# Order of the first steps in a fused attention, router and expert kernel

## What is computed

```python
n  = layernorm(x)                                   # used as a factor on the scores
qp = ctx @ Wq.T + bq;  kp = ctx @ Wk.T + bk         # (4, 512, 128)
s  = (qp @ kp.T) * H ** -0.5 * n                    # (4, 512, 512)
s  = where(mask | key_padding_mask, -inf, s)
x  = x + softmax(s)
t  = layernorm(x).reshape(2048, 512)
shared = silu(t @ sg) * (t @ su) @ sd               # inner width 256
top_val, top_idx = top_k(t @ router_w, 2)
p  = sigmoid(top_val) at top_idx, else 0
out = sum over experts e of (silu(p_e*t @ gate_e) * (p_e*t @ up_e)) @ down_e
x  = x + shared + out
```

## Time and profile before

| what | us |
|---|---|
| median of 3 runs | 363.01 |
| lowest and highest | 361.55, 363.92 |
| the profiled execution | 363.71 |
| its span, first to last instruction | 362.0 |

### The profile page before, as it was taken

How to read it: one execution, slowest core, us unless ns; L and a number is a source line. 1 busy time by engine, 2 the same in 40 slices (tenths; PEclk the granted TensorE clock), 3 DMA queues, 4 the chain that set the end, 5 groups by cost and what they waited for, 6 DMA issues and landing times.

```text
span 362.0 us, 6464 instructions
## 1 busy us (share of the span) xinstructions
PE 318.5 (88%) x1601; PEld 218.8 (60%) x1627; DVE 210.0 (58%) x461; ACT 177.9 (49%) x400; POOL 230.9 (64%) x199
## 2 busy tenths in 40 slices
PE   2866999999999983628999989999999999999991
PEld 1333666676767762315776757777777777777760
DVE  0766789999998789612444334444444444444441
ACT  2477767757767736102644434444444444444440
POOL 0688999986774749958385554756555465555433
PEclk9989899999999998587999999999999999999997
DMA  7956777857556320075346465867666566675736
GB/s 178 308 197 211 206 228 254 247 194 230 205 162 210 124 89 0 0 199 164 68 82 111 72 116 111 131 113 130 108 116 115 115 120 117 91 133 88 132 36 83
DMA packets 29764, 50.61 MB, mean 140 GB/s; under 512 B 5473, under 2 KB 9313, under 8 KB 29729
## 3 DMA queue, kind: packets, MB, share of 16 engines
q0 software_dynamic: 9008, 21.66, 33.5%
q1 hardware_dynamic: 19232, 27.99, 24.6%
q10 hardware_dynamic: 1488, 0.54, 0.8%
HBM read 30.45 MB, written 19.73 MB: 139 GB/s over the span
## 4 chain that ended last, share of the span: by engine, by line
PE 56%; DMA 11%; issue 11%; POOL 9%; DVE 7%; ACT 4%; POOLq 1%; ACTq 0%; DVEq 0%
PE bank L949 10%; PE bank L959 9%; PE bank L954 9%; DMA out_rows<-y,jscatter 9%; PE bank L982 5%; PE bank L988 5%; PE bank L985 5%; PE bank L1073 4%; PE bank L968 3%; POOL gu_lo L356 2%; PE bank L912 2%; POOL pen L351 2%; DMA kpad_in<-in_mask_BxS_bf 2%; PE bank L921 1%; POOL rstd L332 1%
## 5 line engine op out<-in xcount | busy, mean ns | idle before, releaser
L439 POOL DMA_INDIRECT out_rows<-y,jscatter x39 | 61.9, 1588 | 73.3 <-DMA out_rows<-y,jscatter 47.1
L959 PE MATMUL bank<-gu_hi,x_lo 128*128 (+1 forms) x220 | 70.3, 441 | 0.0
L949 PE MATMUL bank<-gu_hi,x_hi 128*128 (+1 forms) x220 | 63.0, 409 | 3.4 <-POOL dn_lo L356 1.4
L671 DVE TENSOR_TENSOR x_lo<-bank,x_hi 128x512 fp32r<-128x512 f32 x55 | 37.9, 690 | 33.1 <-ACT x_bf L507 33.0
L954 PE MATMUL bank<-gu_lo,x_bf 128*128 (+1 forms) x201 | 54.8, 387 | 1.3 <-issue 0.2
L864 DVE SCALAR_TENSOR_TENSOR h<-bank,xg,h 128x256 f32<-128x256 f32 x39 | 18.9, 484 | 57.8 <-ACT h L595 57.8
L420 POOL DMA_INDIRECT xg<-xn_rows,jgather x39 | 41.7, 1069 | 15.5 <-issue 15.5
L514 ACT CAST h_hi<-bank 128x256 fp32r<-128x256 f32 x55 | 20.6, 375 | 59.6 <-PE bank L968 59.4
L959 PEld LDWEIGHTS bank<-gu_hi,x_lo 128*128 128x128 f32 x220 | 41.7, 190 | 12.8 <-issue 0.6
L356 POOL TENSOR_TENSOR gu_lo<-stage,gu_hi 128x1024 bf16<-128x1024 f32 x18 | 43.3, 2405 | 9.6 <-ACT gu_hi L493 9.6
L949 PEld LDWEIGHTS bank<-gu_hi,x_hi 128*128 128x128 f32 x220 | 41.0, 193 | 13.6 <-issue 3.0
(11 more groups left out here) (128 smaller groups left out, 497.5 us busy)
## 6 DMA issues: line engine op xcount, KB each, us to landing
stage<-in_L_ffn_gate_up_w SPq DMA_DIRECT2D x16, 512.0 KB, 3.8
xin<-in_x SPq DMA_DIRECT2D x16, 256.0 KB, 4.3
xn_rows<-xn SPq DMA_DIRECT2D x16, 256.0 KB, 4.0
stage<-in_L_ffn_down_w SPq DMA_DIRECT2D x8, 512.0 KB, 3.8
out_rows<-x SPq DMA_DIRECT2D x16, 256.0 KB, 4.3
out_rows<-zeros POOLq DMA_DIRECT2D x1, 1024.0 KB, 5.0
ctx_in<-in_ctx SPq DMA_DIRECT2D x1, 768.0 KB, 8.6
xg<-xn_rows,jgather POOLq DMA_INDIRECT x39, 4.3
```

Source lines behind the costliest of these rows:

```text
L439: g.indirect_dma_start(out=out, out_offset=bass.IndirectOffsetOnAxis(ap=jscatter[:, n - TILES:n - TILES + 1], axis=0), in_=y[:, r, :], in_ ...
L671: v.tensor_tensor(x_lo[:, n % TS], rows_T(n), x_hi[:, n % TS].bitcast(f32), ALU.subtract).then_inc(xlo_s, 1)
L949: tn.matmul(ps_g(n)[:], x_hi[:, n % TS, k, :], gu_hi[:, e, k, :], start=(k == 0), stop=False)
L959: last = tn.matmul(ps_g(n)[:], x_lo[:, n % TS, k, :], gu_hi[:, e, k, :], start=False, stop=(k == KC - 1))
```

## The change

Nothing is computed otherwise; what each engine does, in which step, is changed, and a few matmuls that compute nothing are added.

- `chunks(s)` follows a table: chunks 0 and 1 in step 0, 2 in step 1, none in step 2, 3 in step 3, then two a step in steps 4 to 9 (4 to 15), and one a step in steps 10 to 14 (16 to 20).
- SP: the context of batches 1 to 3 (768 KB) goes from behind x's tile 0 to behind tile 2 and the gate and up weights of the shared expert.
- PE: 8 and 14 transposes of the identity fill the setup. Scores 1 and context transpose 1 change places; context transpose 3 and the projections of batches 2 and 3 go one to three steps later, those of batch 3 to another bank and one in each of steps 3 and 4. Gate-up 0 waits for two low parts instead of three, and for the third context copy; in step 2 the transpose of h waits until six projections are copied.
- ACT: the first cast stands ahead of the first exponential, and the copies and casts follow the same order.
- DVE: `kpad_pen` comes ahead of the statistics of x 0, those of x 1 behind the first maximum, those of x 2 and x 3 at the end of steps 0 and 1. `rw_lo` goes to POOL, into step 2.
- POOL: the first low part stands in the setup. In steps 0 and 1 the inverse deviations come ahead of the penalty. The clearing of the spare rows goes from the setup into step 2.

```diff
+BOUNDS = (0, 2, 3, 3, 4, 6, 8, 10, 12, 14, 16, 17, 18, 19, 20, 21, 21)
-        ps_ctxT = bank[4]
-        ps_proj = bank[5:7]
+        ps_ctxT = [bank[4], bank[4], bank[4], bank[3]]
+        ps_proj = [bank[5:7], bank[5:7], bank[5:7], [bank[3], bank[3]]]
-            return range(2 * s, 2 * s + 2) if s < 6 else range(s + 6, s + 7) if s < TILES - 1 else range(0)
+            return range(BOUNDS[s], BOUNDS[s + 1])
 # SP
-            sp.dma_start(xin[:, 0, :], x_t[0]).then_inc(ld_x[0], 16)
-            sp.dma_start(ctx_in[:, RT:], ctx_rows[:, RT:]).then_inc(ld_ctx, 16)
-            for t in range(1, AHEAD):
+            for t in range(AHEAD):
                 sp.dma_start(xin[:, t, :], x_t[t]).then_inc(ld_x[t], 16)
...
+            sp.dma_start(xin[:, AHEAD, :], x_t[AHEAD]).then_inc(ld_x[AHEAD], 16)
+            sp.dma_start(ctx_in[:, RT:], ctx_rows[:, RT:]).then_inc(ld_ctx, 16)
             sp.dma_start(stage[:, 2], sd_w.rearrange("(k p) d -> p k d", p=P)).then_inc(ld_st[2], 16)
-            for t in range(AHEAD, XS):
-                sp.dma_start(xin[:, t, :], x_t[t]).then_inc(ld_x[t], 16)
+            sp.dma_start(xin[:, AHEAD + 1, :], x_t[AHEAD + 1]).then_inc(ld_x[AHEAD + 1], 16)
 # POOL
             first_inv_std(1)
+            low_part(0)
+
+            def clear_spare_rows():
...
             for s in range(TILES):
...
-                if s + 2 < TILES:
+                if s < LAG:
+                    pair_inv_std(s)
                     penalty(s + 2)
-                for c in chunks(s)[0:1]:
-                    low_part(c)
-                pair_inv_std(s)
-                for c in chunks(s)[1:]:
-                    low_part(c)
+                    low_part(s + 1)
+                else:
+                    if s + 2 < TILES:
+                        penalty(s + 2)
+                    if s == LAG:
+                        pool.wait_ge(rwhi_s, 1)
+                        g.tensor_tensor(rw_lo[:], rw[:], rw_hi[:].bitcast(f32), ALU.subtract).then_inc(rwlo_s, 1)
+                    for c in chunks(s)[0:1]:
+                        low_part(c)
+                    pair_inv_std(s)
+                    for c in chunks(s)[1:]:
+                        low_part(c)
+                if s == LAG:
+                    clear_spare_rows()
 # ACT
             projections(0)
-            ctx_copy(1)
             act.wait_ge(ld_rw, 16)
             a.copy(rw_hi[:], rw[:]).then_inc(rwhi_s, 1)
+            high_part(0)
...
-                if s + 1 < B:
-                    projections(s + 1)
-                if s + 2 < B:
-                    ctx_copy(s + 2)
-                if j >= 0:
+                if s == 0:
+                    high_part(1)
+                    ctx_copy(1)
+                    projections(1)
+                elif s == 1:
+                    high_part(2)
+                    x_high(0)
+                    ctx_copy(2)
+                else:
                     half_tanh(j)
-                for c in chunks(s):
-                    high_part(c)
-                if s >= 1:
+                    if s == 2:
+                        projections(2)
+                        ctx_copy(3)
+                    if s in (3, 4):
+                        projection(3, s - 3)
+                    for c in chunks(s):
+                        high_part(c)
                     x_high(s - 1)
 # DVE
+            v.tensor_scalar(kpad_pen[:], kpad_in[:], MASKED, None, ALU.mult).then_inc(pen_ready, 1)
             x_stats(0)
             x_mean(0)
-            v.tensor_scalar(kpad_pen[:], kpad_in[:], MASKED, None, ALU.mult).then_inc(pen_ready, 1)
-            x_stats(1)
-            x_mean(1)
-            dve.wait_ge(rwhi_s, 1)
-            v.tensor_tensor(rw_lo[:], rw[:], rw_hi[:].bitcast(f32), ALU.subtract).then_inc(rwlo_s, 1)
...
                 neg_max(s)
-                if s + AHEAD < TILES:
+                if s == 0:
+                    x_stats(1)
+                    x_mean(1)
+                if LAG <= s < TILES - AHEAD:
                     x_stats(s + AHEAD)
...
                         x_low(s - 1)
+                    if s < LAG:
+                        x_stats(s + AHEAD)
+                        x_mean(s + AHEAD)
 # PE
+            def keep_busy(count):
+                for _ in range(count):
+                    tn.transpose(bank[2][:, 0:P], ident[:], ident[:])
+
             pe.wait_ge(c_ident, 1)
+            keep_busy(8)
...
             last.then_inc(wT_ps, 1)
+            keep_busy(14)
             ctx_transpose(0)
+            pe.wait_ge(wT_ready, 1)
             projections(0)
+            scores(0)
+            scores(1)
             ctx_transpose(1)
-            scores(0)

             for s in range(TILES):
                 j = s - LAG
-                if s + 1 < B:
-                    projections(s + 1)
-                if s + 2 < B:
-                    ctx_transpose(s + 2)
+                if s == 0:
+                    projections(1)
+                    ctx_transpose(2)
+                if s in (3, 4):
+                    projection(3, s - 3)
                 if j == 0:
+                    pe.wait_ge(ctxT_ready, 3)
+                    pe.wait_ge(lo_s, 2)
+                if j == 1:
                     pe.wait_ge(lo_s, 3)
...
+                if s == 2:
+                    projections(2)
                 if s >= 1:
                     xn_transpose(s - 1)
-                if s + 1 < TILES:
+                if 1 <= s < TILES - 1:
                     scores(s + 1)
+                if j == 0:
+                    pe.wait_ge(proj_ready, 6)
                 if 0 <= j < FIRST - 1:
                     h_transpose(j)
                     logits(j)
+                if j == 0:
+                    ctx_transpose(3)
```

More of the change, by code:

```diff
@@ L363, in _ @@
             first_inv_std(1)
[L364 to L367, removed]
+            low_part(0)
+            def clear_spare_rows():
+                g.memset(zeros[:], 0.0).then_inc(zero_s, 1)
+                pool.wait_ge(zero_s, 1)
+                g.dma_start(out_t[TILES:TILES + XS].rearrange("r p d -> p r d"),
+                            zeros[:].unsqueeze(1).to_broadcast([P, XS, D])).then_inc(st_trash, 16)
             def late_low(c):
@@ L477, in ctx_copy, with projection @@
                     act.wait_ge(proj_ps, 2 * (b - 1))
-                a.copy(ctxT[:, b % 2, :], ps_ctxT[:]).then_inc(ctxT_ready, 1)
+                a.copy(ctxT[:, b % 2, :], ps_ctxT[b][:]).then_inc(ctxT_ready, 1)
+            def projection(b, w):
+                act.wait_ge(proj_ps, 2 * b + w + 1)
+                a.activation((qT, kT)[w][:, b * S:(b + 1) * S], ps_proj[b][w][:], ACT.Identity, bias=bqk[:, w:w + 1],
+                             scale=SCALING if w == 0 else 1.0).then_inc(proj_ready, 1)
             def projections(b):
[L481 to L484, removed]
+                projection(b, 0)
+                projection(b, 1)
             def expo(s):
@@ L895, in ctx_transpose, with projection @@
                 for r in range(RT):
-                    last = tn.transpose(ps_ctxT[:, r * P:(r + 1) * P], ctx_in[:, b * RT + r, :], ident[:])
+                    last = tn.transpose(ps_ctxT[b][:, r * P:(r + 1) * P], ctx_in[:, b * RT + r, :], ident[:])
                 last.then_inc(ctxT_ps, 1)
-            def projections(b):
-                if b == 0:
-                    pe.wait_ge(wT_ready, 1)
-                pe.wait_ge(ctxT_ready, b + 1)
-                for w in range(2):
-                    if b:
-                        pe.wait_ge(proj_ready, 2 * b - 1 + w)
-                    tn.matmul(ps_proj[w][:], wqkT[:, w, :], ctxT[:, b % 2, :], start=True, stop=True).then_inc(proj_ps, 1)
+            def projection(b, w):
+                pe.wait_ge(ctxT_ready, b + 1)
+                if b:
+                    pe.wait_ge(proj_ready, 2 * b + w if b == B - 1 else 2 * b - 1 + w)
+                tn.matmul(ps_proj[b][w][:], wqkT[:, w, :], ctxT[:, b % 2, :], start=True, stop=True).then_inc(proj_ps, 1)
+            def projections(b):
+                projection(b, 0)
+                projection(b, 1)
             def scores(t):
```

2 lines of the change are left out of this document (1 added, 1 removed).

## The result

The changed kernel takes 367.83 us (median of 4 runs, 365.28 to 370.96) against 363.02 for the kernel before in the same comparison; the ratio is 1.0107 (95% interval 1.0077 to 1.0138), so it is slower by 1.1%, 3.9 us; the medians themselves lie 4.8 us apart. The forecast was 365.0, 2.0 us slower, with a range of 360.3 to 368.0.

A forecast was written before the change was run, and what follows sets the result against it. TensorE was taken to bound the kernel, with POOL pacing two-chunk steps. The profiled 363.71 us plus 2.0 (middle of 1.2 and 2.7) gave 365.7, or 365.0 as a median, that execution lying 0.7 above it; range 360.3 to 368.0.

The forecast's parts named there:

- What bounds: TensorE: gate-up j (tile j's gate and up matmuls) every 6.68 us from 6 on; earlier gain or loss carried unchanged.
- a changed distance from gate-up 10 to the end: Sign of a wrong forecast: the stretch behind tile 10's gate and up matmuls changes, which no term accounts for.
- Steps 4 to 9: Two chunks a step: POOL needs 45.5 us, TensorE 40.1; the 5.4 us exceed the lead, gate-up 10 1.2 to 2.7 late.
- The front: Start through step 4: first exponential 2.8 us earlier, partly lost in waits; gate-up 2 1.3 to 2.7 us ahead.
- rival B: Slower: TensorE's clock falls twice more, over gate-ups 0 and 1, 1.7 us each; median 367.6, chance 0.2.
- The clock: TensorE at half speed in early steps: lower end never after the start, upper for batch 1's projections and gate-up 0.
- Costed at nothing: Other edits free: clearing of spare rows, added bank for last projections, and weight loads one and a half steps ahead.
- rw_lo: Moved to POOL in step 2: taken as 0.3 us; 2.2 by the skill's rule, making the forecast 1.9 us later.
- Rival A: Faster: POOL not starved in steps 1 to 3, idle under about 6 us until step 10; median 360.3, chance 0.17.
- Rival C: Nothing: two-chunk steps hidden, POOL's lateness just meets the lead; median 362.5 to 363.5, chance 0.13.

The follow-up runs named there:

- e5: Changed kernel with chunks alternating 2, 1, 2, 1 from step 3 to 14; median 366.94 us, ratio to before 1.0084.
- e1: Kernel before with only the change's new chunk table; median 364.26 us, ratio to before 1.0032.
- e7: Kernel before with only the table changed, chunks alternating 2, 1, 2, 1 from step 3 to 14; 361.26 us, ratio to before 0.9949.
- e8: Changed kernel with ACT's x_high between a step's first and second cast instead of behind both; 368.22 us, ratio to before 1.0136.
- e10: Changed kernel with four penalties on POOL instead of sixteen, leaving out the key padding masks of batches 1 to 3; 363.38 us, ratio to before 1.0004.
- e9: Changed kernel with rw_lo on POOL in the setup, behind the second penalty, instead of in step 2; 364.92 us, ratio to before 1.0062.
- e2: Changed kernel with chunks moved forward, two a step from step 2 to 6, then one; 368.15 us, ratio to before 1.013.
- e3: Changed kernel without the 22 transposes of the identity; 366.24 us, ratio to before 1.0128.
- e4: Changed kernel with the last context transpose directly behind the projections of batch 2, ahead of the logits; 363.27 us, ratio to before 1.0035.
- e6: Changed kernel with both the alternating table of e5 and the early context transpose of e4; 362.49 us, ratio to before 0.9987.
- e12: e6 with rw_lo in the setup and without the identity transposes; 360.17 us, ratio to before 0.9921.
- e11: e7 with kpad_pen directly behind mask_pen on DVE and rw_lo on POOL in the setup; 360.74 us, ratio to before 0.9942.

## Why the prediction was right, and where its size was off

- **What bounds.** That what is lost up to gate-up 10 is carried on held as far as it goes: gate-up 10 was 3.9 us late, and the eleventh gather's transpose still was. That it is carried *unchanged* into the rest did not hold. The profiled execution lost 3.3 us more between 215 and 229 us, and e5, with gate-up 10 in its old place but for 0.3 us, has a median 3.7 us above before. The prediction had named a changed distance from gate-up 10 to the end as a sign of being wrong, and had no term for it. So the part of the 4.8 us between the medians that is not gate-up 10's lateness stays open, and how much the table costs in time inside the changed kernel is not shown by the medians (e5).
- **Steps 4 to 9.** The term that decided, six POOL periods of together 45.5 us from nmr 4 on, measured 45.50 (45.61 in e1). The step from nmr to gate-up, taken as 3.9, was 3.77. E5 and e7 show that it is the run of two-chunk steps, and the steady rows of nmr together with e8 and e10 that POOL sets its pace, with the loop of ACT and DVE, at 7.16 us a step, right behind.
- **The front.** This is the term that was mis-sized. I gave gate-up 2 as 42.6 to 44.0 and nmr 4 as 51.6 to 53.1; they were 45.42 and 54.31, 1.4 and 1.2 us beyond my late ends. Each of the waits was named, and summed to 10.8 us at most; they were 13.0. The largest part missing is probably the half clock over gate-up 1 and the projection ahead of it, which I had put into rival B; gate-up 1 to gate-up 2 took 8.96 us with it, and 7.77 in e9 without. Rival B as a whole, two falls over gate-ups 0 and 1 and a median of 367.6, gives the time best. Its number is partly luck: it has no loss behind gate-up 10, and gate-up 0 had a full clock (26.04, 1.20 us): the two falls were over the projections of batch 1 and over gate-up 1.
- **The clock.** Gate-up 1 stood at half clock in 4 of the 6 profiled kernels that have the context transpose behind the logits and rw_lo in step 2 (changed, e2, e5, e8; not e3 and e10), and in none of the four that changed one of them or both (e4, e6, e9, e12). In the order of before it stood there once, with the old table, and not in e1, e7 and e11. TensorE waits there for rw_lo and then for ctxT, with logits of 8 columns between. That the waits bring the fall on is what these rows suggest; no run changed the clock alone.
- **Costed at nothing.** The weight loads, which I said keep their distance, do come late for two casts (0.9 us together in the changed kernel, 1.4 in e1). E8 shows that in the changed kernel this is not what costs. Where one such wait was longer, 1.2 to 1.4 us in e1, e3 and e9, TensorE waited for x_high and ran at half clock after it; in e9 that was made up by gate-up 10, in e1 it cost 1.8 us. The clearing of the spare rows was not tried alone.
- **rw_lo.** It took 0.26 us on POOL, as estimated (0.3). The rule of the Trainium skill, GPSIMD Engine Reference, section 4.1 Engine selection, of about twice VectorE's time, would have given 2.2, an estimate from DVE's 1.09, and that did not come. It is no clean test of the rule: DVE's 1.09 us ran beside a penalty on POOL and ended with it, so they need not be VectorE's own time. The price of moving it was not its length but its place, behind a low part of 2.4 us: 1.6 us in e9.
- **Rival A** fell: POOL was idle 13 us, not under 6. **Rival C** fell with it.

From the ratios: the table alone +1.2 us (e1), the context transpose behind the logits 2.6 us (changed against e4, 1.0107 to 1.0035), rw_lo in step 2 1.6 us (e9), of which a part is the same, since both hang on the one context copy. The intervals of changed and e4 are apart; those of changed and e9 overlap. By the medians the three are 1.5, 4.6 and 2.9 us. They don't add up to exactly 3.9 or 4.8, since the terms share the waits in step 2 and the clock, and the late gather is in some of them.

## What to carry to other kernels

Count an engine's work in each step against the step's length at the bound, not over the whole stretch. Here two chunks a step cost 7.3 to 7.9 us on POOL beside 6.7 on TensorE, and six such steps in a row lost 5 us of lead in e1 (1.8 of them by a long wait for weights and a clock fall), while 2, 1, 2, 1 with the same total lost none. Then check the far end as well: a kernel can have its even rhythm back in the old place and still be 3.7 us longer (e5). A small product that the whole queue waits for belongs where it is ready early; its length is not its price.

## What the runs showed that I had not expected

- The fill of 22 transposes did raise TensorE's clock from the first projections on and brought the first exponential 2.4 us forward, with no gain seen in the end; the clock was at half again at 16 us, after 3.6 us of waiting.
- DVE's rw_lo took 1.09 us and POOL's 0.26 us for the same 128x32 elements. DVE's (13.68 to 14.77) ended together with a penalty on POOL, in the kernel before; what held it was not tried.

```profile
13.58 1.14 POOL L351 TENSOR_TENSOR pen<-mask_pen,kpad_pen 128x512 bf16<-128x512 bf16 x1
```

- The order of casts on ACT (e8) changed who waits for whom, six waits for nmr instead of two, and the length of the eight tiles by nothing.
